# An attention and MLP layer on one core: the prologue reordered around a transposed x, and the sparse branch moved into the first head

## The chip, the cores and the metric

The program runs on one core of one Trainium2 chip. The metric is the device time of one execution in microseconds (us), as the median of several. Five engines run their own instruction streams and meet at semaphores: PE (TensorE, matmuls and transposes; PEld is its weight load), DVE (VectorE), ACT (ScalarE), POOL (GpSimd) and SP (SyncE), which here issues the DMAs. [...]

## What is computed

One transformer layer on x, 1024 tokens by 256 features, in float32:

```python
qc = layernorm(x @ W_cq, q_norm_w, q_norm_b)            # query latent, 192 wide
qp = qc @ W_q                                           # 16 heads x (128 nope + 64 rope)
kvc = x @ W_ckv                                         # 16 heads x (64 rope + 128)
kv_n = layernorm(kv_nope, kv_norm_w, kv_norm_b)
kvp = kv_n @ W_kv                                       # k_nope and v
attn = softmax(causal(q k^T * scale)) @ v               # per head, rope on q_pe and k_pe
gate = x @ W_ig;  top 8 tokens for each of 8 side heads # sparse branch
sel = rows of (x @ W_ip) at those tokens
so = softmax(sel W_sq (sel W_sk)^T / sqrt(128)) @ (sel W_sv)
attn += mean over the 8 tokens of (so @ W_io)           # one vector per side head
x = layernorm(x + attn @ W_o)
x = layernorm(x + MLP(x) with ternary weights)
```

The sparse branch gives one vector per head, the same for all tokens, so it enters the output as one row that is summed over the heads and added to all tokens.

## The kernel before

Every float32 product is made of two float32r halves, a high part (ACT or POOL rounds it, names ending in h) and a low part (DVE or POOL subtracts it, names ending in l), so a logical matmul is three matmuls (`three`, L610 to L612) and nearly every result needs an ACT copy and a DVE subtraction (the helper `lo`, L943). x is 8 tiles of 128 tokens; xTh and xTl hold its transpose in two blocks of 128 features.

Order is written by hand. One list of steps, `PROLOGUE`, then `FIRST` (heads 0 and 1), `MID` in a loop (pairs 1 to 6), `LAST` (heads 14 and 15) and `EPILOGUE` is walked by each engine, which does its own share of each step in list order and waits on semaphores for the others. A step that needs an accumulator takes one of four PSUM banks J in turn and PE waits until its last user has been read out. The scores of a head go to the two large PSUM tensors SC. Each head has 8 slots, one per query tile: `qk` (scores, L623 to L627), some filler steps, `exp`, more filler steps (transposes of the probabilities `tc`, products with v `pv`, output product `wo`, and the preparation of the next head: `kpe`, `kv`, `kvn`, `kvn2`, `kt`, `qp`, `ab`, `qn`, `ropek`, `ropeq`, `stk`, `stq`).

In the prologue the steps are: `xt` (16 PE transposes of x, L696), `qc` (the query latent and the gate for each token tile; ACT copies it out in three pieces, DVE takes statistics, L1022 and L1026), `qrs` (POOL, 1/sqrt of the variances of all 8 tiles), `kpe` and `kv` (key rope part and key/value latent of heads 0 and 1), `ropek` (POOL, L503 to L512, after a DMA swaps even and odd rows of KX), `qnorm` (DVE normalises the latent in SBUF, 16 instructions, L1033), `ab` (products of weights), `qm` (PE transposes the normalised latent; ACT scales, rounds; DVE subtracts), `side` 0 and 1 (gate transposed, top 8 by DVE), `qp`, `qn` (queries), `kvn2` and `kt` (keys of head 0), `ropeq` on DVE, and then `side` 2 to 10, the sparse branch, a chain that goes from PE to DVE and back at each of nine steps. Step 3 (L663) picks the chosen rows of x with 16 float32 matmuls of 64 columns, step 4 (L671) multiplies them by W_ip with 16 of 8 columns. At its end `rw` (the row of head 0) precedes the first `qk`. SP's DMAs `stack` copy the roped keys and queries to the doubled layouts KD, KL and QS that `qk` reads.

## Time and profile before

| | us |
|---|---|
| median of 3 executions | 739.39 (738.97 to 739.40) |
| the profiled execution | 743.51 |
| its span | 741.7 |
| first scores of head 0 (start of L623) | 84.96 |
| PE busy over the span | 670.4 (90%) |
| DVE / ACT / POOL busy | 490.9 / 397.5 / 338.9 |

The numbers of the trace are from one profiled execution, 743.51 us long, of which 741.7 us are its span; the median is 4.1 us less than that execution. Times of instructions are counted from the start of the span. In a timeline row, the first number is the start, the second the duration of the group, and what stands in brackets is the idle time before it on its engine and who ended it.

### The profile page before, as it was taken

What the parts mean: (1) busy time and instruction counts of PE and PEld (TensorE: products, weight loads), DVE (VectorE), ACT (ScalarE), POOL (GpSimd) and SP (SyncE); (2) the same over time, 40 slices, a digit from 0 to 9 for tenths busy, and PEclk for the clock granted to TensorE, in tenths of its full rate; (3) what the DMA queues carried; (4) which work ended last, traced back from release to release, by engine and by line L of the source; (5) the groups of instructions that cost most, each with busy time, mean ns of one, the idle gap of its engine ahead of it and who ended that gap; (6) DMA issues with size and microseconds to landing.
All of it is one profiled execution on the core that took longest, in us unless ns stands there. A gap on an engine that the chain in (4) does not pass through costs nothing. (4 is left out here: it accounts for less than half of the span.)

```text
span 741.7 us, 14057 instructions
## 1 busy us (share of the span) xinstructions
PE 670.4 (90%) x4416; PEld 600.9 (81%) x4416; DVE 490.9 (66%) x1401; ACT 397.5 (54%) x920; POOL 338.9 (46%) x279
## 2 busy tenths in 40 slices
PE   5667799999999999999999999999999999878994
PEld 5546699889988898899889988998899889767883
DVE  2665366666676666666766676667666668996665
ACT  3341345764576457645764476447644766644531
POOL 5622354735474547354735474547454730000443
PEclk9965599999999999999999999999999999998998
DMA  6153210551045105510541055105410545000001
GB/s 200 44 141 72 64 50 1 124 112 51 1 103 134 50 0 120 113 50 0 125 108 50 0 127 106 50 0 129 104 50 0 127 86 171 1 0 1 1 1 57
DMA packets 29486, 50.50 MB, mean 68 GB/s; under 512 B 8976, under 2 KB 20496, under 8 KB 29456
## 3 DMA queue, kind: packets, MB, share of 16 engines
q1 hardware_dynamic: 29456, 50.12, 27.0%
q8 instruction: 16, 0.26, 0.1%
q14 instruction: 14, 0.11, 0.1%
HBM read 15.50 MB, written 1.05 MB: 22 GB/s over the span
## 5 line engine op out<-in xcount | busy, mean ns | idle before, releaser
L943 DVE TENSOR_TENSOR PTl<-J,PTh 128x512 fp32r<-128x512 f32 (+1 forms) x192 | 102.2, 553 | 65.3 <-ACT PTh L832 64.7
L845 ACT ACTIVATE Pb<-SC,nm 128x128 f32<-128x128 f32 (+7 forms) x128 | 94.8, 740 | 62.9 <-DVE nm L1010 62.9
L1006 DVE CUSTOM_DVE_ANT_0 SC<-SC,mask 128x128 f32<-128x128 f32 (+7 forms) x128 | 97.3, 760 | 28.0 <-PE SC L627 25.8
L610 PE MATMUL J<-PTh,Vh 128*128 128x256 f32 x320 | 88.3, 276 | 7.0 <-DVE PTl L943 6.8
L636 PE MATMUL J<-ident,Pb 128*128 128x128 f32 x576 | 88.1, 279 | 6.0 <-ACT Pb L845 5.5
L612 PE MATMUL J<-PTh,Vl 128*128 128x256 f32 x320 | 89.3, 279 | 0.0
L611 PE MATMUL J<-PTl,Vh 128*128 128x256 f32 x320 | 89.3, 279 | 0.0
L832 ACT ACTIVATE PTh<-J 128x512 fp32r<-128x512 f32 (+1 forms) x192 | 87.5, 493 | 2.6 <-PE J L636 1.7
L636 PEld LDWEIGHTS J<-ident,Pb 128*128 128x128 f32 x576 | 63.8, 141 | 13.8 <-ACT Pb L845 5.4
L610 PEld LDWEIGHTS J<-PTh,Vh 128*128 128x128 f32 x320 | 60.7, 190 | 11.7 <-DVE PTl L943 10.4
L623 PE MATMUL SC<-KNh,QNh 128*128 128x512 f32 (+1 forms) x192 | 69.0, 360 | 0.0
L624 PE MATMUL SC<-KNl,QNh 128*128 128x512 f32 (+1 forms) x192 | 66.8, 348 | 0.0
L625 PE MATMUL SC<-KNh,QNl 128*128 128x512 f32 (+1 forms) x192 | 66.8, 348 | 0.0
L626 PE MATMUL SC<-KD,QS 128*128 128x512 f32 (+1 forms) x192 | 66.7, 347 | 0.0
L627 PE MATMUL SC<-KL,QS 128*128 128x512 f32 (+1 forms) x192 | 66.6, 347 | 0.0
L832 ACT ACTIVATE ATh<-J 128x256 fp32r<-128x256 f32 x64 | 24.5, 383 | 69.6 <-PE J L612 68.9
L611 PEld LDWEIGHTS J<-PTl,Vh 128*128 128x128 f32 x320 | 60.6, 189 | 0.7
L612 PEld LDWEIGHTS J<-PTh,Vl 128*128 128x128 f32 x320 | 60.9, 190 | 0.0
L1143 DVE SCALAR_TENSOR_TENSOR acc<-J,rs,acc 128x256 f32<-128x256 f32 x128 | 56.1, 480 | 2.6
L943 DVE TENSOR_TENSOR ATl<-J,ATh 128x256 fp32r<-128x256 f32 x64 | 27.0, 422 | 45.1 <-ACT ATh L832 45.0
L907 ACT ACTIVATE kvraw<-kvraw,nmr,rstd 128x128 f32<-128x128 f32 x128 | 52.5, 485 | 5.0 <-POOL nmr L589 5.0
L832 ACT ACTIVATE kvraw<-J 128x512 f32<-128x512 f32 x32 | 19.2, 599 | 65.8 <-PE J L612 65.8
(283 smaller groups left out, 1869.9 us busy)
## 6 DMA issues: line engine op xcount, KB each, us to landing
KD<-RKh SPq DMA_DIRECT2D x32, 256.0 KB, 4.5
KL<-RKl SPq DMA_DIRECT2D x32, 256.0 KB, 5.0
KX<-KX SPq DMA_DIRECT2D x16, 256.0 KB, 2.4
QX<-QX SPq DMA_DIRECT2D x16, 256.0 KB, 2.3
QS<-RQh SPq DMA_DIRECT2D x16, 256.0 KB, 4.0
QS<-RQl SPq DMA_DIRECT2D x16, 256.0 KB, 4.5
r_kv<-in_L_attn_W_ckv SPq DMA_DIRECT2D x8, 384.0 KB, 3.4
r_qn<-in_L_attn_W_qT SPq DMA_DIRECT2D x16, 128.0 KB, 2.8
```

The source lines that it names most:

```text
L610: mm(o, lhsT=wh, rhs=xh, start=start, stop=False)
L611: mm(o, lhsT=wh, rhs=xl, start=False, stop=False)
L612: return mm(o, lhsT=wl, rhs=xh, start=False, stop=stop)
L623: mm(o[:, k], lhsT=QNh[b][:, q], rhs=KNh[b][:, k], start=True, stop=False)
L624: mm(o[:, k], lhsT=QNh[b][:, q], rhs=KNl[b][:, k], start=False, stop=False)
L625: mm(o[:, k], lhsT=QNl[b][:, q], rhs=KNh[b][:, k], start=False, stop=False)
L626: mm(o[:, k], lhsT=QS[b][:, q], rhs=KD[b][:, k], start=False, stop=False)
L636: last = pe.transpose(o[:, tile(j - 4 * c)], Pb[i % 2][:, tile(j)], ident[:, :])
L832: return act.activation(o, i, ACT.Copy)
L845: act.activation(Pb[i % 2][:, w], SC[i % 2][:, w], ACT.Exp, bias=nm[:, i % 2:i % 2 + 1], scale=SCALE, accum_out=sm[:, b, i:i + 1]).then_in ...
L943: dve.tensor_tensor(o, i, h.bitcast(F32), ALU.subtract).then_inc(done[kind], 1)
L1006: dve.tensor_tensor_reduce(out=SC[i % 2][:, w], in0=SC[i % 2][:, w], in1=mask[:, 128 * (7 - i):S], scale=1.0, scalar=LOW, op0=ALU.add, op1 ...
```

## The change

1. The host also passes x transposed (xT), the six vectors of the two norms as one array (vec), W_cq with W_ig beside it, cos and sin as one array, and the rope columns of W_q packed for one DMA. The 16 transposes and their 4 copies disappear; xT is loaded in two halves of 512 tokens into KX, one half by SP and one by ACT's own DMA queue, which also loads cos/sin and x. Step `xs` rounds a half (ACT, 128x1024) and subtracts (DVE, 128x1024).
2. `qc` writes into SC, not into J, and is not copied out. Its statistics, `qrs` and `qnorm` are done in halves of four tiles. The first half is normalised by ACT (8 instructions out of PSUM), the second by DVE (8 instructions out of PSUM), both into QX. `qm` follows by halves.
3. The scaling of W_kvT by the norm weights and the splits of W_kvT and of the first W_q and W_o block go from POOL to a new step `w0` on ACT (copies) and DVE (one multiplication and three subtractions). It stands ahead of `kv` 0 and of the second half of `qnorm`.
4. `ropek` 0 keeps three operations on POOL; its copy and subtraction become step `rsplit` on ACT and DVE. `ropeq` 0 is done in halves on DVE with its own swap and stack DMAs.
5. Steps `side` 2 to 10 and `io` leave the prologue for the slots of head 0. The row of head 0 (`rw`) is done in the last pair, for which W_o's first block is loaded a second time.
6. Buffers of the sparse branch move from Pb to QX and Pb[1], so ACT waits for `side` 4 before it writes KX for pair 1, and for `side` 10 before it writes QX for it.

```diff
-            sp.dma_start(acc[:, :, :], x.rearrange("(t p) d -> p t d", p=128)).then_inc(ld_x, 16)
-            sp.dma_start(ident[:, :], c_ident).then_inc(ld_x, 16)
...
+            sp.dma_start(r_cq, W_cqg.rearrange("(k p) n -> p k n", p=128)).then_inc(ld_cq, 16)
+            sp.dma_start(KX[:, :, half(0)], xT.rearrange("(k p) n -> p k n", p=128)[:, :, half(0)]).then_inc(ld_xt[0], 16)
...
+            act.dma_start(KX[:, :, half(1)], xT.rearrange("(k p) n -> p k n", p=128)[:, :, half(1)]).then_inc(ld_xt[1], 16)
+            act.dma_start(CS[:, :, :], c_cs).then_inc(ld_cs, 16)
+            act.dma_start(acc[:, :, :], x.rearrange("(t p) d -> p t d", p=128)).then_inc(ld_x, 16)
...
                     if kind == "qrs":
-                        inv_std(qmv[:, :, 1], ve[:, :], rsd[:, :], qc_aggr, 1, qc_veps, qc_rstd, 1)
+                        q = slice(4 * c, 4 * c + 4)
+                        inv_std(qmv[:, q, 1], ve[:, q], rsd[:, q], qc_aggr, c + 1, qc_veps, qc_rstd, c + 1)
...
+                    if kind == "qnorm" and c == 0:
+                        act.wait_ge(qc_neg, 2)
+                        for t in range(4):
+                            v = qc_out(t)
+                            act.activation(qcm[:, t, :], v[:, 0:128], ACT.Identity, bias=nmr[:, t:t + 1], scale=rsd[:, t:t + 1])
+                            act.activation(qct[:, t, :].rearrange("p (a n) -> p a n", a=2),
...
+                    if kind == "w0":
+                        act.wait_ge(wkv_scaled, 1)
+                        copy(Wkh[:, :], r_wkv).then_inc(hi_w, 1)
+                        act.wait_ge(ld_qn, 16)
+                        copy(Wqnh[:, :, :], r_qn[:, :, :]).then_inc(wqn_hi, 1)
+                        act.wait_ge(ld_o, 16)
+                        copy(Woh[:, :], r_o[:, :]).then_inc(wo_hi, 1)
...
                     if kind == "qnorm":
-                        dve.wait_ge(qc_rstd, 1)
-                        dve.wait_ge(qc_aggr, 1)
-                        for t in range(T):
-                            for v in (qcm, qct):
-                                ins = dve.tensor_scalar(v[:, t, :], v[:, t, :], qmv[:, t, 0:1], rsd[:, t:t + 1],
...
+                    if kind == "w0":
+                        dve.wait_ge(ld_w0, LD_W0)
+                        dve.tensor_tensor(r_wkv[:, NOPE:], r_wkv[:, NOPE:], kvwr, ALU.mult).then_inc(wkv_scaled, 1)
+                        dve.wait_ge(hi_w, 1)
+                        dve.tensor_tensor(Wkl[:, :], r_wkv, Wkh[:, :].bitcast(F32), ALU.subtract).then_inc(w0_ready, 1)
...
+                add(0, first, ("side", 0, 2))
+                add(1, first, ("side", 0, 3))
+                add(2, first, ("side", 0, 4))
+                add(3, first, ("side", 0, 5), ("side", 0, 6))
+                add(4, first, ("side", 0, 7))
+                add(5, first, ("side", 0, 8))
+                add(5, last, ("wosp", 2, 0), ("io0", 0, 0))
+                add(6, first, ("side", 0, 9))
+                add(7, first, ("side", 0, 10), ("io", 0, 0))
+                add(7, last, ("rw", 2, 0))
```

The order on DVE in the prologue, before, from the statistics of the key/value latent to the low part of the first transposed query latent (Pb here holds the means, rsd the inverse deviations):

```order
L1046 BN_STATS bst<-kvraw 128x6 [waits kv_done]
L1046 BN_STATS bst<-kvraw 128x6 x3
L1033 TENSOR_SCALAR QX<-QX,Pb,rsd 128x128 [waits qc_aggr,qc_rstd]
L1033 TENSOR_SCALAR QX<-QX,Pb,rsd 128x128 x15
L1054 BN_AGGR mv<-bst 128x2 [waits bn_done]
L1054 BN_AGGR mv<-bst 128x2 x15
L943 TENSOR_TENSOR ABl<-J,ABh 128x512 [waits ab_hi]
L943 TENSOR_TENSOR qcl<-J,qch 128x512 [waits qm_hi] x2
```

And now, from the low parts of the first half to the second half of the normalisation (Pb<-Pb is the scaling of W_kvT; Wkh, Wqnh and Woh are the high parts that ACT rounds):

```order
L1012 TENSOR_TENSOR qcl<-J,qch 128x512 [waits qm_hi]
L1012 TENSOR_TENSOR qcs<-J,qcs 64x512 [waits qm_hi]
L1121 TENSOR_TENSOR Pb<-Pb 128x128 [waits ld_w0]
L1123 TENSOR_TENSOR Wkl<-Pb,Wkh 128x256 [waits hi_w]
L1125 TENSOR_TENSOR Wqnl<-r_qn,Wqnh 128x256 [waits wqn_hi]
L1127 TENSOR_TENSOR Wol<-r_o,Woh 128x256 [waits wo_hi]
L1135 BN_STATS bst<-kvraw 128x6 [waits kv_done]
L1135 BN_STATS bst<-kvraw 128x6 x3
L1106 TENSOR_SCALAR QX<-SC,Pb,rsd 128x128 [waits qc_aggr,qc_rstd]
L1108 TENSOR_SCALAR QX<-SC,Pb,rsd 128x128
```

Four operations on two SBUF inputs now stand on DVE ahead of the second half of the normalisation, which reads PSUM (SC); they were POOL's.

PE before, ahead of head 0: steps 2 to 5 of the sparse branch in one row (Pb holds the one-hot matrix and then the picked rows, KX holds W_ip):

```order
L658 MATMUL J<-i8d,onesf 128x64 [waits side_dve,qn_done]
L663 MATMUL J<-Pb,acc 128x64 [waits side_dve,qn_done]
L663 MATMUL J<-Pb,acc 128x64 x15
L671 MATMUL J<-Pb,KX 128x8 [waits ld_wip,side_done,kt_done]
L671 MATMUL J<-Pb,KX 128x8 x15
L675 MATMUL J<-Pb 128x64 [waits side_done,kt_done]
```

PE now, in the slots 0 to 2 of head 0 (SC rows are its scores, ident,Pb the transposed probabilities):

```order
L668 MATMUL SC<-KL,QS 128x128
L701 MATMUL J<-i8d,onesf 128x64 [waits side_dve,qn_done]
L664 MATMUL SC<-KNh,QNh 128x256
L665 MATMUL SC<-KNl,QNh 128x256
L666 MATMUL SC<-KNh,QNl 128x256
L667 MATMUL SC<-KD,QS 128x256
L668 MATMUL SC<-KL,QS 128x256
L677 MATMUL J<-ident,Pb 128x128 [waits exp_done,qn_done]
L707 MATMUL J<-QX,acc 128x64 [waits ld_x,side_dve,kt_done]
L707 MATMUL J<-QX,acc 128x64 x15
L664 MATMUL SC<-KNh,QNh 128x384 [waits exp_done]
```

The same matmuls of the sparse branch are issued, but after the first scores and between them, in PE's in-order queue.

## Rows read from the trace of the kernel before

**Rows 1.** Timeline of PE, 0 to 85 us: start, duration, engine, line, operation

```profile
6.70 3.67 PE L696 MATMUL J<-ident,acc 128*128 128x128 f32 x16 [6.70 <-DMA ident<-in_c_ident]
...
11.87 0.50 PE L610 MATMUL J<-KNh,xTh 128*128 128x200 f32 x1 [1.50 <-DVE xTl L943]
...
17.73 0.39 PE L610 MATMUL J<-KNh,xTh 128*128 128x200 f32 x1
...
40.87 3.65 PE L709 MATMUL J<-ident,QX 128*128 128x128 f32 x16 [10.81 <-DVE QX L1033]
...
61.41 7.06 PE L663 MATMUL J<-Pb,acc 128*128 128x64 f32 x32 [3.86 <-DVE Pb L969]
68.90 6.96 PE L671 MATMUL J<-Pb,KX 128*128 128x8 f32 x32 [0.43 <-issue]
...
81.03 0.35 PE L683 MATMUL J<-mean,Pb 64*64 64x8 f32 x2 [1.56 <-DVEq L989]
...
84.96 0.31 PE L623 MATMUL SC<-KNh,QNh 128*128 128x128 f32 x1
```

**Rows 2.** Timeline of ACT, 0 to 80 us

```profile
23.20 0.60 ACT L832 ACTIVATE KX<-J 128x512 f32<-128x512 f32 x1 [0.80 <-PE J L612]
...
52.68 3.17 ACT L907 ACTIVATE kvraw<-kvraw,nmr,rstd 128x128 f32<-128x128 f32 x8
```

**Rows 3.** Timeline of POOL, 0 to 80 us

```profile
26.98 2.40 POOL L503 TENSOR_TENSOR KX<-KX,CS 128x1024 f32<-128x1024 f32 x1 [2.90 <-issue]
...
31.77 2.34 POOL L506 TENSOR_TENSOR KX<-KX 128x1024 f32<-128x1024 f32 x1
...
42.28 2.92 POOL L554 TENSOR_TENSOR rstd<-veps,mhalf 128x16 f32<-128x16 f32 x1
...
59.99 0.72 POOL L548 TENSOR_TENSOR Wqnl<-r_qn,Wqnh 128x256 fp32r<-128x256 f32 x1
```

**Rows 4.** Groups by shape, POOL 714 to 742 us, DVE 600 to 665 us: busy, mean ns

```profile
L1226 POOL TENSOR_TENSOR rsd<-ve,mhalf 128x4 f32<-128x4 f32 x2 | 2.0, 1007 | 0.2
...
L1132 DVE TENSOR_TENSOR acc<-acc,row 128x512 f32<-128x512 f32 x4 | 2.6, 683 | 0.0
```

**Rows 5.** Timeline of DVE, 0 to 80 us

```profile
25.25 0.87 DVE L1046 BATCH_NORM_STATS2 bst<-kvraw 128x6 f32<-128x128 f32 x4 [3.27 <-ACT kvraw L832]
...
30.48 10.24 DVE L1033 TENSOR_SCALAR QX<-QX,Pb,rsd 128x128 f32<-128x128 f32 x16
40.65 1.15 DVE L1054 BATCH_NORM_AGGREGATE mv<-bst 128x2 f32<-128x6 f32 x16
...
47.95 1.28 DVE L951 COPY QX<-J 8x512 f32<-8x512 f32 x2
...
52.02 0.21 DVE L962 TENSOR_TENSOR i8d<-i8f,blk 8x64 f32<-8x64 f32 x1
56.37 1.29 DVE L943 TENSOR_TENSOR QNl<-J,QNh 128x512 fp32r<-128x512 f32 x2 [4.14 <-ACT QNh L832]
...
60.24 1.02 DVE L969 TENSOR_TENSOR Pb<-Pb,tokid 128x512 f32<-128x512 f32 x1
61.18 1.21 DVE L503 TENSOR_TENSOR QX<-QX,CS 128x1024 f32<-128x1024 f32 x1
...
65.76 1.23 DVE L512 TENSOR_TENSOR RQl<-QX,RQh 128x1024 fp32r<-128x1024 f32 x1
```

**Rows 6.** The instructions of L1033, 30 to 41 us: ns min/median/max

```profile
L1033 DVE TENSOR_SCALAR QX<-QX,Pb,rsd x16: 330/334/2501, 30.5 to 40.4; 128x128 f32<-128x128 f32 x16
```

**Rows 7.** DMA issues of the page: KB each, us from issue to landing

```profile
KL<-RKl SPq DMA_DIRECT2D x32, 256.0 KB, 5.0
```

**Rows 8.** Busy time by stretch: PE, PEld, DVE, ACT, POOL, granted clock, DMA

```profile
61.40:75.90 14.50, 14.03 (x64) 13.78 (x64) 5.57 (x7) 0.00 (x0) 0.00 (x0) 0.50 0.53 120
84.90:89.30 4.40, 4.20 (x18) 3.88 (x17) 1.87 (x8) 1.78 (x7) 3.45 (x4) 0.50 0.00 2
89.30:122.00 32.70, 32.20 (x222) 29.41 (x221) 20.35 (x57) 18.17 (x40) 17.54 (x14) 0.99 0.09 29
```

More of the change, by code:

```diff
@@ L317, in head_steps @@
             else:
+                add(0, first, ("rw", h, 0), ("wosp", n, 0))
                 add(0, more, ("qp", 1, 0), ("kvn", 1, 0))
@@ new lines, in _ @@
+            load("wkv", 0)
+            sp.dma_start(vecs[:, :], vec).then_inc(ld_vec, 16)
+            sp.dma_start(ident[:, :], c_ident).then_inc(ld_id, 16)
+            load("wqp", 0)
+            sp.dma_start(r_wkv, W_kvT).then_inc(ld_w0, 16)
+            sp.dma_start(r_wv, W_kv[:, NOPE:]).then_inc(ld_w0, 16)
+            sp.dma_start(kvwr, kv_norm_w.rearrange("(a n) -> a n", a=1).to_broadcast([128, NOPE])).then_inc(ld_w0, 16)
+            load("wqn", 0)
+            load("wosp", 0)
+            for dst, src in ((blk[:, :], c_blk), (tokid[:, :], c_tok), (off64[:, :], c_off), (mean8[:, :], c_mean)):
@@ L467, in _ @@
             sp.dma_start(wip, W_ip.rearrange("(k p) n -> p k n", p=128)).then_inc(ld_wip, 16)
-            stack("stk", 0, 0, 0)
-            sp.wait_ge(side_dve, 2)
-            swap(QX, done["qp"], 2, q_swapped)
-            stack("stq", 0, 0, 0)
+            for n, src in enumerate((W_sq, W_sk, W_sv, W_io[:, 0:128])):
+                sp.dma_start(wside[:, n, :], src).then_inc(ld_ws, 16)
             def run(steps, p):
@@ L506, in rope @@
             eng.tensor_tensor(X[:, 0, :], X[:, 0, :], X[:, 1, :], ALU.add).then_inc(mul, 1)
-            eng.wait_ge(mul, 4 * u + 3)
-            for b in range(2):
-                hold(eng, stacked[b], 96 * u)
+            eng.wait_ge(mul, 4 * n + 3)
+            if isinstance(u, int) and u == 0:
+                return
+            hold(eng, stacked[0], 96 * u - 32)
+            hold(eng, stacked[1], 96 * u)
             eng.tensor_copy(hi_[:, :], X[:, 0, :]).then_inc(mul, 1)
-            eng.wait_ge(mul, 4 * u + 4)
+            eng.wait_ge(mul, 4 * n + 4)
@@ L691, in use @@
                 b = off % 2
-                if kind == "xt":
-                    if c == 0:
-                        pe.wait_ge(ld_x, 32)
-                    for t in range(4):
-                        last = pe.transpose(o[:, tile(t)], acc[:, 4 * (c % 2) + t, tile(c // 2)], ident[:, :])
                 if kind == "qc":
                     if c == 0:
-                        pe.wait_ge(w0_ready, 1)
-                        pe.wait_ge(done["xt"], 4)
+                        pe.wait_ge(cq_ready, 1)
+                    if c % 4 == 0:
+                        pe.wait_ge(done["xs"], c // 4 + 1)
+                    o = qc_out(c)
                     for k in range(K):
-                        last = three(o[:, 0:200], xTh[:, k, tile(c)], xTl[:, k, tile(c)], Wcqh[:, k, :], Wcql[:, k, :],
+                        last = three(o[:, :], xTh[:, k, tile(c)], xTl[:, k, tile(c)], Wcqh[:, k, :], Wcql[:, k, :],
                                      k == 0, k == K - 1)
@@ L846, in run @@
                                        scale=SCALE, accum_out=sm[:, b, i:i + 1]).then_inc(exp_done, 1)
-                    if kind in ready and kind not in ("side", "wb", "wtot", "wo", "rw"):
+                    if kind in ready and kind not in ("side", "wb", "wtot", "wo", "rw", "qc"):
                         act.wait_ge(ready[kind], count(kind, u, c))
@@ L893, in run @@
+                    if kind == "rsplit":
+                        act.wait_ge(rk_mul, 3)
+                        copy(RKh[:, :], KX[:, 0, :]).then_inc(rk_mul, 1)
                     if kind == "kpe":
@@ L911, in run @@
                             wait(act, rq_ready, u)
+                        if c == 0 and isinstance(u, int) and u == 1:
+                            act.wait_ge(done["side"], 11)
                         copy(QX[:, 0, half(c)], o[:, :]).then_inc(done["qp"], 1)
@@ L1408, with attn, two @@
-    for name, a in constants().items():
-        arrays[f"in_{name}"] = np.ascontiguousarray(a)
+    args = []
+    a = {name: np.ascontiguousarray(v) for name, v in inputs.items()}
+    def attn(name):
+        return a[f"L0_attn_{name}"]
+    def two(v):
+        return np.concatenate([v, v])
+    x = attn("x").reshape(S, D)
+    qw, qb = attn("q_norm_w"), attn("q_norm_b")
+    heads = attn("W_q").reshape(QL, NP, 2, HD)
+    pe = heads[:, :, :, NOPE:].transpose(1, 0, 2, 3).reshape(NP, QL, 128)
@@ L1410 @@
+    for name in ("W_o", "W_ip", "W_sq", "W_sk", "W_sv", "W_io"):
+        arrays[f"in_{name}"] = attn(name)
+    for name in ("W_up", "W_gate", "W_down"):
+        arrays[f"in_{name}"] = a[f"L0_ffn_{name}"]
+    for name, v in constants().items():
+        arrays[f"in_{name}"] = v
+    arrays = {name: np.ascontiguousarray(v) for name, v in arrays.items()}
     for name, a in arrays.items():
```

324 lines of the change are left out of this document (184 added, 140 removed).

## The prediction

> **What bounds the kernel now.** I read the windows by stretch first, then PE's timeline, then the other engines around PE's gaps. From 89.3 us on PE is the bound: 32.20 of 32.70 us busy at a granted clock of 0.99 [rows 8], and the heads after it repeat that. So a microsecond of PE work added to a head is paid in full, and a microsecond by which head 0 begins sooner is won in full. Head 0 begins at 84.96 [rows 1]. Ahead of it PE waits in two places. First, 10.81 us for the normalised query latent: DVE takes 10.24 us for 16 small instructions [rows 5]. Second, the sparse branch, from 61.41 to 84 us. Of that, 7.06 + 6.96 us are the matmuls of steps 3 and 4, in which PE is 14.03 of 14.50 us busy, but at a granted clock of 0.50 [rows 1, 8]. The rest, about 9 us, is small steps handed to and fro.
>
> So the sum has two parts: when head 0 now begins, and by how much it gets longer.
>
> **Part 1: the begin of head 0.** *Start.* PE's 16 transposes began at 6.70 when x and ident had landed, and `qc` at 11.87 [rows 1]. xT's first half lands with 1.2 MB in flight, as x and ident did, so at 6 to 7 us; I take 7.0. ACT rounds 1024 columns (1.0 to 1.2 us, two copies of 512 at 0.60 [rows 2]), DVE subtracts 1024 (1.23 [rows 5]); `qc` begins at 9.7, some 2 us sooner.
>
> *First half of the latent.* 27 matmuls of `qc` took 5.86 us [rows 1], so 24 take 5.2: 14.9. Statistics of the last two tiles and the aggregation take 1.2 more by estimate: 16.1. POOL's power on 4 columns takes 1.0 [rows 4], with three small operations around it 1.9 by estimate: 18.0. ACT's 8 scalings cost 3.17 as those of `kvn2` [rows 2]: 21.5 with the gate copy. `kpe` is copied out behind them: 22.7 (before 23.80). The swap DMA and its wait took from 23.80 to 26.98 [rows 2, 3], so POOL's three rope operations begin at 25.9 and hold POOL until about 33.4 (three of 2.34 to 2.40 [rows 3]).
>
> *Step w0, the term that decides.* DVE finishes the low parts of `qm` 1 at 26.1 (two scalings and copies on ACT) and meets four operations with both inputs in SBUF, each 0.3 to 0.45 alone (128 and 256 columns, where 512 take 0.683 [rows 4]). The trace shows what POOL does to such work. In `qnorm` the 16 instructions have a median of 0.334 us and a longest of 2.501 [rows 6]; they took 10.24 together [rows 5] while POOL's rope ran from 26.98 on [rows 3]. L969, two SBUF inputs of 512 columns, began at 60.24, while POOL's L548 ran until 60.71; it took 1.02, where an operation of this size takes 0.683 with POOL idle [rows 3 to 5]. It ended 0.55 us after POOL's operation did, which is what its 512 elements alone need. So such an operation waits for the end of POOL's. The first of the four therefore ends at 28.4, ACT's three copies follow by 29.6, the second ends at 31.1, the third at 33.9, the fourth at 34.3. Alone the four would be through at 28.0.
>
> [...]
>
> *Second half.* Behind the four stand the statistics of `kv` 0 (0.87 [rows 5]) and `qnorm` (8 out of PSUM; from 0.33 each, as when unhindered in SBUF, overlapped to 0.3; 2.4 in all, 5 if each took twice that): 37.6. PE has been idle since about 24 and is at the lower clock. It then has 8 transposes, `kv` 1, `qp` 0, `kv` 2, `qp` 1, `kv` 3 in one row. With 0.22 a matmul at the lower clock at first (16 took 3.65 [rows 1]) and the upper clock from about 42 (as it rose at 89.3 after dense work from 84.2 on [rows 8]), that ends at 47.3.
>
> *DVE's chain.* Copy 0.6, statistics 0.9, aggregation 1.15 [rows 5]: 50.1. ABl 0.65 (half of QNl's 1.29 [rows 5]). The top 8, from 47.95 to 52.23 before [rows 5], 4.3: 55.1. Rope of the first query half, half of 61.18 to 66.99 [rows 5], 3.0: 58.1, plus 0.6 behind POOL's split of v. QNl 1.3 [rows 5]: 60.1. RKl 1.2 and about 1 behind POOL again: 62.4. The key path on POOL and ACT (power 2.92, scalings 3.17 [rows 2, 3]) ends sooner. SP then issues four stack DMAs, the last 1.9 later; it lands in 5.0 [rows 7]: **69.4**. Before, the stacks were hidden by the sparse branch; here nothing hides them. Won: 84.96 - 69.4 = **15.6 us**.
>
> **Part 2: head 0 gets longer.** *Steps 3 and 4.* PE stands idle from about 58 (the last transposes of `kt`) to 69.4, so head 0 opens at 0.50, as it did before [rows 8]. Two sets of scores (2.3 us) precede step 3. In the trace 14 us of these very matmuls left the clock at 0.50 [rows 8]. I take them at 7.06 + 6.96 = 14.0; at the upper level they would cost half. *Small steps.* Step 2 is 0.4; steps 5 to 10 are 14 matmuls of 0.11 (half of 7.06/32): 1.6. *Waits.* Step 6 waits for DVE to copy step 5, behind ABl: 1.6. Step 8 waits for the side softmax (DVE, ACT, DVE), which was 1.56 of idle PE before [rows 1] and stands ahead of `kv` and `pv` in PE's queue: 1.6. *Clock.* The scores and transposes between steps 3 and 4 now also run at the lower level, some 4 us of them: 2.0. Sum: 14.0 + 0.4 + 1.6 + 3.2 + 2.0 = **21.2 us**. The bounds are 10 (everything at the upper level, waits filled) and 25 (waits doubled).
>
> **Elsewhere.** `rw` goes from the prologue to the last pair: three matmuls and a DVE row, 0.35. POOL's W_o split now precedes `kvn` in head 1: at most 1.2, I take 0.3. The packed loads save SP issue time, which nobody waits for. The waits of ACT on step 4 and step 10 come after these in PE's order anyway. Together **+0.6**.
>
> **Sum.** -15.6 + 21.2 + 0.6 = +6.2 against the profiled 743.5, so 749.7 for such an execution. That one stood 4.1 over the median, so the median goes from 739.4 to **745.6**. Its own error, from 2 us at the start and in DVE's chain and 3 in head 0, gives 741 to 750. A difference of 0.2% (1.5 us) is about what a measurement can tell from none.
>
> **Rivals.**
> *A. The four operations of w0 aren't hindered* (they slip in ahead of POOL's rope or don't share its port). Then `qnorm` 1 ends at 31.5, RKl isn't held either: head 0 begins 7.5 sooner, +6.2 - 7.5 = -1.3, 738.1. For it: only one row of this kind of operation. Against: that row fits to 0.1 us. Chance 0.12.
> *B. Steps 3 and 4 run at the upper level.* It saves 7.0 there and about 2.5 of the scores: -3.3, 736.1. For it: in head 0 they have dense scores beside them. Against: at 61.4 to 75.9 the clock stayed at 0.50, and here it begins low. Chance 0.14.
> [...] The trace shows the clock low through 14 us of these matmuls.
> *C. Both*: +6.2 - 7.5 - 9.5 = -10.8, 728.6. Chance 0.06.
> *D. Head 0 suffers more*: the side softmax blocks DVE and with it the maxima of the scores; if each of the nine steps costs a wait like 1.56, 5 to 8 more, 752. It decides once exp of tile 5 arrives after PE has run out of `kv` work. Against: DVE is 20.35 of 32.70 us busy there [rows 8]. Chance 0.06.
> That leaves 0.62 for the forecast.
>
> **How the numbers follow.** Range 734.5 to 750.5: it leaves out C, the lower end of B and nearly all of D. The bounds of step 3 and 4 (half price) and of w0 (alone) are in it each by itself. Faster by over 0.2%: C 0.06, B 0.11, A 0.05, forecast 0.02 = 0.24. Within 0.2%: B 0.02, A 0.04, forecast 0.05 = 0.11. Slower: 0.65. The likeliest case alone: 741 to 750.
>
> **What would show it.** In the changed trace: L647 from about 9.7; POOL L522 to L525 at 26 to 33 with DVE L1123 or L1125 lasting 2 us beside them; L1106/L1108 unhindered, ending near 37.6; the first L664 at 67 to 72, released by a stack DMA; L707 and L715 of 7 us each at 0.50; PE idle before L723 and L728 of over 1 us each; head 1's first scores about 21 us further from head 0's than before. If the first L664 comes at 62, A holds; if L707 takes 3.5 us, B does. Not covered: a wait in the loop of the middle pairs, whose order is unchanged.

## The result and the profile after

| | before | after |
|---|---|---|
| median (us) | 739.39 (738.97 to 742.97, 4 executions) | 750.36 (749.26 to 750.85, 4 executions) |
| profiled execution, its span | 743.51, 741.7 | 750.04, 748.3 |
| first scores of head 0 / head 1 / head 15 | 84.96 / 120.26 / 630.07 | 72.08 / 129.27 / 637.66 |

The ratio of the times is 1.0136, 95% interval 1.0108 to 1.0163: the changed kernel is 1.4% slower. Head 0 begins 12.9 us sooner and is 57.2 us long instead of 35.3, so head 1 begins 9.0 us later. That lead shrinks to 7.6 at head 15 and to 6.6 at the end of the span.

The start of the prologue, from the timelines of ACT, DVE and PE (start, duration, engine, line, operation; in brackets the idle time before it and who ended it):

```profile
10.19 2.00 ACT L882 ACTIVATE xTh<-KX 128x1024 fp32r<-128x1024 f32 x2 [6.62 <-DMA KX<-in_xT]
...
11.28 2.99 DVE L1012 TENSOR_TENSOR xTl<-KX,xTh 128x1024 fp32r<-128x1024 f32 x2 [11.28 <-ACT xTh L882]
...
12.65 0.51 PE L647 MATMUL SC<-KNh,xTh 128*128 128x200 f32 x1 [12.65 <-DVE xTl L1012]
```

x transposed lands at 10.2, not at 7, so `qc` begins at 12.65: 0.8 us later than before (11.87 in [rows 1]), although the 16 transposes are gone.

Step w0, from the timeline of DVE, and POOL in the same stretch:

```profile
28.26 2.27 DVE L1121 TENSOR_TENSOR Pb<-Pb 128x128 f32<-128x128 f32 x1
31.02 2.01 DVE L1123 TENSOR_TENSOR Wkl<-Pb,Wkh 128x256 fp32r<-128x256 f32 x1 [0.48 <-ACT Wkh L882]
32.95 2.56 DVE L1125 TENSOR_TENSOR Wqnl<-r_qn,Wqnh 128x256 fp32r<-128x256 f32 x1
35.43 0.41 DVE L1127 TENSOR_TENSOR Wol<-r_o,Woh 128x256 fp32r<-128x256 f32 x1
35.76 0.86 DVE L1135 BATCH_NORM_STATS2 bst<-kvraw 128x6 f32<-128x128 f32 x4
36.66 0.41 DVE L1106 TENSOR_SCALAR QX<-SC,Pb,rsd 128x128 f32<-128x128 f32 x1
...
28.05 2.34 POOL L522 TENSOR_TENSOR KX<-KX,CS 128x1024 f32<-128x1024 f32 x1 [4.64 <-issue]
30.35 2.40 POOL L523 TENSOR_TENSOR KX<-KX,CS 128x1024 f32<-128x1024 f32 x1
32.82 2.40 POOL L525 TENSOR_TENSOR KX<-KX 128x1024 f32<-128x1024 f32 x1
```

Put the two engines side by side: L1121 ends at 30.53 and POOL's L522 at 30.39; L1123 at 33.03 and L523 at 32.75; L1125 at 35.51 and L525 at 35.22. Each of DVE's began while one of POOL's ran and ends 0.1 to 0.3 us behind it. L1127, of the same size as L1125, has POOL idle beside it and takes 0.41 instead of 2.56.

From there to head 0, the timelines of DVE and PE show:

```profile
39.54 1.94 PE L753 MATMUL J<-ident,QX 128*128 128x128 f32 x8 [12.91 <-DVE gts L1111]
...
51.40 1.29 DVE L1145 BATCH_NORM_AGGREGATE mv<-bst 128x2 f32<-128x6 f32 x16
...
62.73 2.17 DVE L1130 TENSOR_TENSOR RKl<-KX,RKh 128x1024 fp32r<-128x1024 f32 x1
...
72.08 0.45 PE L664 MATMUL SC<-KNh,QNh 128*128 128x128 f32 x1 [11.06 <-DMA KL<-RKl]
```

PE waits 12.91 us for the second half of the latent (before: 10.81, for the whole of it [rows 1]), and 11.06 us ahead of the first scores, for the stack DMA of RKl.

The timeline of PE in head 0:

```profile
75.36 6.93 PE L707 MATMUL J<-QX,acc 128*128 128x64 f32 x32
84.22 6.83 PE L715 MATMUL J<-QX,KX 128*128 128x8 f32 x32
...
100.79 0.41 PE L723 MATMUL J<-QX 128*64 128x128 f32 x2 [1.38 <-DVE QX L1048]
111.10 0.25 PE L728 MATMUL J<-mean,QX 64*64 64x8 f32 x2 [2.07 <-DVEq L1061]
```

And busy time by stretch (stretch, length, PE, PEld, DVE, ACT, POOL, granted clock, DMA share, GB/s):

```profile
75.30:91.00 15.70, 15.70 (x74) 15.60 (x73) 2.24 (x9) 3.43 (x10) 5.99 (x4) 0.50 0.64 152
91.00:96.00 5.00, 5.00 (x17) 4.29 (x17) 2.20 (x5) 2.58 (x4) 0.00 (x0) 0.50 0.00 0
...
98.00:125.00 27.00, 23.55 (x154) 20.61 (x153) 16.30 (x48) 10.58 (x25) 12.66 (x9) 1.00 0.11 35
```

Steps 3 and 4 (L707, L715) cost what they cost before (7.06 and 6.96, [rows 1]), at the same clock of 0.50, the lower of the two values (0.50 and 1.00) that the clock records of this case's 14 traces have. They stood ahead of head 0 and now stand in it.

### The profile page after: what moved, and what is told of

The parts are those of the page before. It is cut to its first block and busy times, and to the rows that moved or that the text cites. A ratio compares the mean times of both kernels' runs of the same rounds, so it can differ in the third digit from the quotient of the medians.

```text
span 748.3 us, 13998 instructions
## 1 busy us (share of the span) xinstructions
PE 664.8 (89%) x4400; PEld 596.8 (80%) x4400; DVE 494.8 (66%) x1403; ACT 397.5 (53%) x907; POOL 337.2 (45%) x276
## 3 DMA queue, kind: packets, MB, share of 16 engines
q1 hardware_dynamic: 24512, 48.68, 25.9%
## 5 line engine op out<-in xcount | busy, mean ns | idle before, releaser
L664 PE MATMUL SC<-KNh,QNh 128*128 128x512 f32 (+1 forms) x192 | 69.6, 363 | 11.1 <-DMA KL<-RKl 11.1
L522 POOL TENSOR_TENSOR KX<-KX,CS 128x1024 f32<-128x1024 f32 x8 | 19.1, 2386 | 77.7 <-DMA KX<-KX 73.1
```

The lines of the kernel that those rows point to most:

```text
L664: mm(o[:, k], lhsT=QNh[b][:, q], rhs=KNh[b][:, k], start=True, stop=False)
```

## The experiments

The times of the kernel before in these comparisons are from new executions on the same chip as each group. Its median was 740.2 to 741.5 there, and 739.4 beside the changed kernel. So a difference of medians between two such groups can be off by 1 to 2 us; the ratio to the kernel before doesn't have this error. The groups are: the kernel before once more, w0 earlier, loads later and the sparse branch ahead again (740.70); both edits, steps 2 to 4 ahead, the added matmuls and the 80 at the start (740.23); step 3 alone ahead and the last two rows of the table (741.51); the kernel before with PE occupied (741.05).

| kernel | median | ratio to before, 95% | head 0 begins | head 1 begins |
|---|---|---|---|---|
| before, once more | 740.42 | 1.0007 (0.9983 to 1.0031) | 82.66 | 118.36 |
| before, PE occupied from 1.4 us | 740.38 | 0.9988 (0.9971 to 1.0005) | 82.23 | 118.26 |
| after | 750.36 | 1.0136 (1.0108 to 1.0163) | 72.08 | 129.27 |
| w0 earlier | 742.75 | 1.0026 (1.0002 to 1.0049) | 63.95 | 120.78 |
| loads later | 747.19 | 1.0084 (1.0056 to 1.0111) | 68.93 | 126.08 |
| 80 matmuls added at the start | 755.73 | 1.0194 (1.0151 to 1.0237) | 78.47 | 135.03 |
| steps 3, 4 once more in head 1 | 756.18 | 1.0209 (1.0177 to 1.0240) | 70.62 | 125.47 |
| sparse branch ahead again | 750.87 | 1.0142 (1.0096 to 1.0189) | 92.23 | 127.67 |
| w0 and loads | 739.29 | 0.9979 (0.9964 to 0.9995) | 60.86 | 119.23 |
| and steps 2, 3 ahead of head 0 | 735.52 | 0.9922 (0.9906 to 0.9939) | 64.71 | 114.47 |
| and steps 2, 3, 4 ahead of head 0 | 732.44 | 0.9897 (0.9864 to 0.9930) | 68.71 | 110.41 |
| and step 3 ahead of kt | 728.48 | 0.9822 (0.9806 to 0.9839) | 65.16 | 108.74 |
| and PE occupied at the start | 726.92 | 0.9798 (0.9773 to 0.9823) | 62.86 | 106.50 |

### Step w0 moved ahead of POOL's rope

```diff
-  each("qc", 4, 5, 6, 7) + each("qrs", 1) + ... + each("qm", 0, 1) + each("w0", 0) + each("kv", 0)
+  each("w0", 0) + each("qc", 4, 5, 6, 7) + each("qrs", 1) + ... + each("qm", 0, 1) + each("kv", 0)
```

> Only the place of step w0 changes: its DVE and ACT work stands between the fourth and the fifth tile of the query latent, where POOL is idle, and no longer behind qm 1 beside POOL's rope of the shared key. Theory (DVE's instructions with two SBUF inputs wait for POOL's of 2.4 us): the four take 0.3 to 0.45 each, the second half of the latent is normalised by about 32 instead of 39.3, head 0's first scores come at 65 to 66 instead of 72.1, time 743 to 745 (-6 to -7). Rival (the cost is the handing to and fro between ACT and DVE in w0, wherever it stands): the later steps of the query latent are pushed back by as much, head 0 at 71 to 73, time 749 to 751. The second rival: head 0 comes sooner but the stacks or POOL's key path are late next: head 0 at 68 to 70, time 746 to 748.

The timelines of DVE and POOL in this kernel, then PE's first scores:

```profile
18.27 0.26 DVE L1121 TENSOR_TENSOR Pb<-Pb 128x128 f32<-128x128 f32 x1
19.01 0.43 DVE L1123 TENSOR_TENSOR Wkl<-Pb,Wkh 128x256 fp32r<-128x256 f32 x1 [0.49 <-ACT Wkh L882]
19.36 0.42 DVE L1125 TENSOR_TENSOR Wqnl<-r_qn,Wqnh 128x256 fp32r<-128x256 f32 x1
19.69 0.42 DVE L1127 TENSOR_TENSOR Wol<-r_o,Woh 128x256 fp32r<-128x256 f32 x1
...
28.66 0.41 DVE L1106 TENSOR_SCALAR QX<-SC,Pb,rsd 128x128 f32<-128x128 f32 x1
...
18.81 1.01 POOL L585 TENSOR_TENSOR rsd<-ve,mhalf 128x4 f32<-128x4 f32 x1
...
27.53 2.34 POOL L522 TENSOR_TENSOR KX<-KX,CS 128x1024 f32<-128x1024 f32 x1 [4.47 <-issue]
29.84 2.34 POOL L523 TENSOR_TENSOR KX<-KX,CS 128x1024 f32<-128x1024 f32 x1
...
63.95 0.45 PE L664 MATMUL SC<-KNh,QNh 128*128 128x128 f32 x1 [11.05 <-DMA KL<-RKl]
```

The same four instructions take 1.5 us together instead of 7.3, the normalisation ends at 31.4 instead of 39.4, and head 0 begins 8.1 us sooner. The time falls by 7.6 (by the ratios, 1.1%). All three lie a little beyond what was forecast, and both rivals fall: nothing else was late behind it. About 0.7 of the 8.1 is not w0's: the first half of the latent was through that much sooner in this trace (DVE's statistics of its last two tiles begin at 17.31, and at 18.01 in the changed kernel).

Two rows say more exactly what hinders whom. POOL wasn't idle in the new place: L1123 and L1125 ran wholly within its L585, which has 4 columns and lasts 1.01 us, and took 0.43 and 0.42. So not every POOL instruction holds DVE up until it ends; the ones that do in these traces have 256 columns or more. (The profile's spans on POOL are rough.) And the eight normalisations out of PSUM ran beside POOL's L522 and L523 here, every 0.32 us as in the changed kernel, where POOL had been idle since 35.22.

### Tables and x loaded behind the rest

```diff
-            act.dma_start(CS[:, :, :], c_cs).then_inc(ld_cs, 16)
-            act.dma_start(acc[:, :, :], x.rearrange(...)).then_inc(ld_x, 16)
...
+            sp.dma_start(CS[:, :, :], c_cs).then_inc(ld_cs, 16)
+            sp.dma_start(acc[:, :, :], x.rearrange(...)).then_inc(ld_x, 16)
             for dst, src in ((blk[:, :], c_blk), ...
```

> The rope tables and x (2.5 MB with the rest) are issued by SP behind its other loads and not on ACT's queue beside the two halves of x transposed. Theory (xT landed at 10.1 and not at 7 since it shared the DMA engines with what nobody needs yet): xT's halves land at 7 to 8, the first copy on ACT begins there, everything up to head 0 moves by 2 to 3 us, time 747.5 to 748.5. Rival (an aggregate limit or the size of xT itself sets 10 us): xT lands at 9.5 to 10.1, time 750 to 751.

Its ACT timeline:

```profile
7.36 2.00 ACT L882 ACTIVATE xTh<-KX 128x1024 fp32r<-128x1024 f32 x2 [4.79 <-DMA KX<-in_xT]
```

xT is there 2.8 us sooner, head 0 begins 3.1 us sooner, and the time falls by 3.2, 0.3 beyond the forecast. The two DMAs of 1 MB each that ACT issued at 1.3 and 1.8 us delayed the one load for which every engine waited. The two traces show it: ACT began on xT at 10.19 with the two DMAs beside it and at 7.36 without. Up to 14 us the queue of ACT's DMAs moved 2.59 MB in the changed kernel and 0.52 MB in this one; SP's half of xT landed 8.9 us after its issue there and 6.1 here.

### The sparse branch ahead of head 0 again

```diff
-                add(0, first, ("side", 0, 2))
-                add(1, first, ("side", 0, 3))
...
-                add(7, first, ("side", 0, 10), ("io", 0, 0))
...
                     each("kt", 0, 1) + each("vs", 0) +
+                    each("side", *range(2, 11)) + each("io", 0) +
```

> Sparse steps 2 to 10 and the initial output return ahead of head 0, all else as in the changed kernel. Theory (the sum of the prediction): head 0 is 35.3 long again instead of 57.2, and begins 22 to 25 us later than 72.1, at 94 to 97, since PE has nothing else beside these steps there; time 748 to 754. So placing them in head 0 gained at most 3 us. Rival 1 (the placement is what costs: waits of DVE and PE in head 0): begins at 84 to 88, time 739 to 744. Rival 2 (the placement gained much): over 756.

Head 0 is 35.4 us long again (92.23 to 127.67), and begins 20.2 us later than in the changed kernel: 750.87 against 750.36. Behind `kt` in this form, the move into head 0 neither wins nor loses. The begin at 92.23 is 1.8 us sooner than the theory had it; the time is in its range. PE stands idle for 8.66 us ahead of step 3, where it was 3.86 before [rows 1]. DVE makes the one-hot matrix only behind the rope of the queries and the low parts of the keys, from 69.82 to 70.51 in this trace:

```profile
70.61 7.06 PE L700 MATMUL J<-QX,acc 128*128 128x64 f32 x32 [8.66 <-issue]
```

### Both edits together

> Both edits together: step w0 ahead of the fifth latent tile, the rope tables and x issued by SP behind its other loads. Theory (both lie in one row ahead of head 0): the gains add, 8.2 and 3.2 us earlier in the traces so far; head 0's first scores at 60 to 61.5, time 739 to 741. Rival (the key path or the stacks take over): KNl and the stack DMAs set the begin at 62 to 63.5, time 741.5 to 743.

Head 0 begins at 60.86, so the gains add (11.2 in the trace of 8.1 + 3.1). The time is 739.29, 0.2% under the kernel before with the interval just below 1, and 11.1 under the changed kernel. With the sparse branch still in head 0, these two placements in the prologue were the whole loss.

### Steps 2, 3 and 4 in PE's idle stretch

W_ip gets 4 KB per partition of its own and the second half of KX (free once POOL has added the rotated part); the one-hot matrix, the indices and the gathered vectors stand in columns of Pb that are free then, so that the steps needn't wait for QX. The three steps leave the slots of head 0, and steps 5 to 10 stay there.

```diff
-        wip = KX[:, :, :]
+        wip0 = sb("wip0", [128, S])
+        wip = [wip0[:, :], KX[:, 1, :]]
...
-        oneh = QX[:, 0, 512:1024].rearrange("p (t n) -> p t n", t=T)
-        idxb = QX[:, 1, 0:64]
+        oneh = Pb[1][:, 512:1024].rearrange("p (t n) -> p t n", t=T)
+        idxb = Pb[0][:, 400:464]
...
-                    each("ab", 0) + each("side", 0, 1) + ...
+                    each("ab", 0) + each("side", 0, 1, 2) + ...
-                    each("kt", 0, 1) + each("vs", 0) +
+                    each("kt", 0, 1) + each("side", 3, 4) + each("vs", 0) +
```

> The two edits before, and sparse steps 2, 3 and 4 ahead of head 0: step 2 directly behind the top 8, steps 3 and 4 behind the last transposes of kt, in the stretch in which PE waits for the stack DMAs; W_ip is loaded early into space of its own and the free half of KX, one-hot, index and gathered vectors stand in free columns of Pb. Steps 5 to 10 stay in head 0. Theory (PE's idle stretch, about 11 us before the first scores, is free for 14 us of matmuls that head 0 would have to carry): head 0 is 40 to 43 long instead of 57, and begins 4 to 7 us later than without the move, at 65 to 68; time 728 to 732. Rival 1 (DVE's two operations for step 2 hold up the rope of the queries and RKl, and the clock is not up sooner): begins at 70 or later, time 733 to 737. Rival 2 (the matmuls in the gap bring the clock up early): head 0 35 to 38 long, time 724 to 727.

Head 0 is 41.7 us long (68.71 to 110.41), where 58.4 stood without the move, and begins 7.9 later (forecast 4 to 7). Together head 1 begins 8.8 sooner in the traces. The median falls by 6.9 to 732.44, 0.4 over the forecast range; the profiled executions were the slowest of the one kernel (740.37) and the fastest of the other (731.59), 8.8 apart. PE's timeline of step 3 and busy time by stretch in this kernel:

```profile
54.88 5.69 PE L710 MATMUL J<-Pb,acc 128*128 128x64 f32 x32 [1.52 <-DVE QNl L1013]
```

```profile
54.90:56.40 1.50, 1.50 (x14) 1.50 (x14) 1.50 (x2) 1.47 (x4) 0.98 (x2) 1.00 0.65 142
56.50:60.50 4.00, 4.00 (x20) 3.88 (x19) 3.75 (x7) 1.00 (x3) 0.00 (x0) 0.50 0.62 125
...
68.70:75.00 6.30, 5.96 (x28) 5.39 (x29) 2.87 (x12) 3.59 (x11) 3.19 (x3) 0.62 1.06 243
75.00:110.40 35.40, 31.43 (x211) 27.91 (x210) 21.19 (x64) 16.18 (x37) 15.54 (x11) 1.00 0.10 31
```

The clock is up within 6 us of the head's begin, where it was down for 24 us in the changed kernel. It fell in the middle of step 3, with PE busy, after a wait of 1.52 us ahead of it.

### The same with step 4 left in head 0

> As all_gap34, but step 4 (16 matmuls of 8 columns) stays in head 0, slot 2; only steps 2 and 3 stand ahead of it. The run with the same shapes in a warm head had step 3's shape at 3.7 us with the clock left at 1.00, and the clock fell to 0.50 in the middle of step 4's shape. Theory (step 4 is what keeps or takes the clock down in head 0): head 0 begins at 62 to 64 and is 48 to 52 long, its clock is not at 1.00 before step 4 has ended, time 735 to 738, 3 to 5 us over all_gap34. Rival (in head 0 step 4 costs only its own 3.5 to 4.5 us, the clock comes up without regard to it): head 0 44 to 46 long, time 730 to 732.

```profile
64.70:80.00 15.30, 15.10 (x63) 14.36 (x64) 3.57 (x13) 6.20 (x16) 5.95 (x4) 0.50 0.64 155
80.00:114.40 34.40, 31.07 (x206) 27.64 (x206) 20.53 (x63) 13.68 (x31) 12.66 (x9) 0.98 0.08 28
```

Head 0 is 49.8 us long, 8.1 more than with step 4 ahead of it, and begins 4.0 sooner. The clock is at 0.50 until step 4 has ended, with PE 15.10 of 15.30 us busy. These are the theory's numbers for the head's length and the clock; the begin at 64.71 is 0.7 later than it had it. The time is 3.1 over that of the run above, at the theory's lower end. That difference is between two groups, and by the ratios (0.9922 and 0.9897, whose intervals overlap) it is not clear of noise; the traces, with head 1 4.1 us later, carry it.

### Steps 3 and 4 in a head at the upper level

The changed kernel, with these shapes issued once more ahead of `kt` and `ab` in head 1; nothing reads them.

```diff
+                if kind in ("kt", "ab") and isinstance(u, int) and u == 2 and c == 0:
+                    pe.wait_ge(ld_cs, 16)
+                    n = 64 if kind == "kt" else 8
+                    for k in range(K):
+                        for t in range(T):
+                            mm(o[:, 64 * k:64 * k + n], lhsT=CS[:, k, tile(t)], rhs=ident[:, 0:n], start=True, stop=True)
```

> The changed kernel with the shapes of sparse steps 3 and 4 once more, in a head in which the clock is at 1.00: 16 float32 matmuls of 64 columns ahead of the kt of head 1's slots and 16 of 8 columns ahead of its ab; nothing reads their results. Theory 1 (they cost PE instructions whose length the granted clock sets, and dense neighbours keep it up): 3.5 us each at a clock of 1.00, head 1 7 us longer than 33.5, time 757 to 758. Theory 2 (such matmuls take the clock down themselves): the clock falls to 0.50 within them or behind them, 7 us each, head 1 12 to 16 us longer, time 762 to 767. Rival 3 (hidden: head 1 has spare time on PE): under 3 us.

PE's timeline, and the clock by stretch:

```profile
137.11 3.68 PE L781 MATMUL J<-ident,CS 128*128 128x64 f32 x32
...
145.34 4.53 PE L781 MATMUL J<-ident,CS 128*128 128x8 f32 x32
```

```profile
137.10:140.70 3.60, 3.60 (x34) 3.59 (x33) 2.19 (x7) 2.08 (x6) 2.68 (x2) 1.00 1.00 219
...
148.00:149.90 1.90, 1.90 (x10) 1.90 (x11) 0.54 (x2) 0.00 (x0) 1.90 (x2) 0.50 0.00 0
149.90:154.00 4.10, 4.10 (x15) 3.62 (x16) 0.69 (x1) 0.60 (x1) 2.39 (x2) 0.50 0.94 204
```

Step 3's shape goes as theory 1 has it, step 4's as theory 2. The shape of 64 columns costs half of what it costs cold (3.68 against 6.93) and leaves the clock at 1.00. In the middle of the shape of 8 columns the clock falls to 0.50 (at 147.9) and stays there through ordinary work until 154.7; PE was busy throughout. Head 1 is 42.8 us long instead of 33.5. The median is 5.8 over that of the changed kernel, less than either theory forecast: in this trace head 0 began 1.5 us sooner and was 2.3 shorter, of which more below. The clock also dipped in head 0 of the kernel with step 3 ahead of `kt` (0.92 at 85 to 90, 0.74 at 90 to 95), beside waits, so this doesn't prove that the 8-column matmuls took it down.

This same trace holds the case of rival B. Its prologue is that of the changed kernel, but the real step 4 ran from 82.76 in 3.76 us, and head 0 was 54.9 us long:

```profile
73.91 6.93 PE L707 MATMUL J<-QX,acc 128*128 128x64 f32 x32
82.76 3.76 PE L715 MATMUL J<-QX,KX 128*128 128x8 f32 x32
```

So the clock can rise there, at the same instruction stream: it did at 83.0 in this trace, and fell again at 86.4, in the last of step 4's matmuls. In five others with the branch in head 0 (after, w0 earlier, loads later, both, 80 matmuls at the start) it didn't rise, and step 4 took 6.83.

### Occupying PE at the start

```diff
+            pe.wait_ge(const_ready, 1)
+            for _ in range(80):
+                mm(J[0][:, 0:128], lhsT=onesf[:, :], rhs=onesf[:, :], start=True, stop=True)
             run(numbered(PROLOGUE), 0, [None] * NB)
```

> The changed kernel with 80 matmuls more (128 x 128, ones by ones, into a bank that is overwritten) on PE from 1.4 us, where it has nothing to do until 12.6. Theory (the changed kernel has lost the 16 transposes of x that ran from 7 to 10.5, so its first 18 latent matmuls, at 0.215 us apiece instead of 0.111, are always cold, as those of the first profile of the kernel before were and those of its second were not): the first latent matmuls come every 0.11 us, everything moves by 1.8 to 2.2 us, time 748 to 749. Rival (the clock has nothing to do with it): same cadence and the same time, 750.4 +- 0.7.

The experiment was mis-sized: each of these float32 matmuls stands in the trace as two passes (160 for the 80), they kept PE until 21.8, and `qc` began at 21.60 instead of 12.65. The time rose to 755.73. It still shows the cadence: the latent of eight tiles took 5.6 us from there, where it took 8.0 in the changed kernel.

The kernel before, with 18 of them:

> The kernel before with 18 matmuls of ones by ones on PE from 1.4 us until its transposes of x begin at about 7. So far its runs lie in two groups, about 739 and about 742 to 743.5; the first profile (743.5) had its first latent tiles 1.28 us apart, the second (739.7) 0.67 apart. Theory (which group a run falls into is set by whether the clock has risen when the latent's first matmuls run): the tiles are 0.67 apart, all runs at 738 to 740, no second group, median 0.5 to 2 us under that of the kernel before on the same chip. Rival (the spread comes from elsewhere, later in the program): two groups as before, the same median within 0.5 us.

Five of 17 executions of the kernel before beside it were over 743 us, and none of its 12 (highest 742.23), but a group at 740 to 742 remains and the medians differ by 0.7, within the interval. The first tiles are fast (a pass every 0.11 us from 12.27 on), but the matmuls also held up the transposes: DVE's first low part is at 9.64, where it was at 8.79 in the second profile of before. That the start divides the two groups of executions is not shown.

### Step 3 ahead of kt, and the same with PE occupied

```diff
-                    each("rsplit", 0) + each("ropeq", 1) + each("kt", 0, 1) + each("side", 3, 4) + ...
+                    each("rsplit", 0) + each("side", 3) + each("ropeq", 1) + each("kt", 0, 1) + each("side", 4) + ...
```

> As all_gap34, with step 3 directly behind the two matmul groups of qn, ahead of kt, and not behind kt. Theory (PE idles between these, and the low part of kt has 2 us to spare before the stacks land): step 3 from 51 to 58, step 4 from 59.5 to 66.5, first scores at 66 to 67 instead of 68.7, time 729.5 to 731. Rival (kt now comes 5 us later, KNl is late and the keys' path sets the begin): 68.5 to 70, time 732 to 733.5.

> best_order with 28 matmuls of ones by ones on PE from 1.4 us (two passes each, so 56 passes: at 0.217 and then 0.115 us they end at 9 to 9.8, where 80 of them ended at 21.8 in the run that had meant to test this and so held the latent up by 9.2 us). Theory (the first latent matmuls are cold): the 48 latent passes take 5.5 us instead of 7.3, all behind them moves by 1.5 to 2 us, time 1.5 to 2 us under best_order. Rival (the pause before xT's low part is ready, or another stretch behind, takes it back): within 0.7 us of best_order.

PE's timeline of the first of these:

```profile
52.04 3.68 PE L710 MATMUL J<-Pb,acc 128*128 128x64 f32 x32
...
65.16 0.45 PE L667 MATMUL SC<-KNh,QNh 128*128 128x128 f32 x1 [0.52 <-DMA KL<-RKl]
```

Head 0 begins 3.6 us sooner than with both steps behind `kt`, more than the 1.7 to 2.7 forecast: directly behind `qn` the clock stays at 1.00 through step 3 (52.0 to 55.7), which takes 3.68 and not 5.69. PE now waits 0.52 us for the last stack, so the two paths to head 0 are level. Head 0 itself got 1.9 us longer (43.6), with the dip of the clock in it that was told above, so head 1 begins only 1.7 us sooner, and the profiled executions are 1.8 apart (731.59 and 729.84). The medians differ by 4.0, across two groups. 728.48 is 1.8% under the kernel before.

With 28 matmuls at the start, the latent is through in 5.6 us. Busy time of its stretch in that kernel:

```profile
9.70:15.40 5.70, 5.70 (x50) 5.66 (x50) 4.47 (x14) 1.03 (x3) 4.69 (x5) 1.00 1.03 376
```

and in the changed one (what its 1.00 means is told at the end):

```profile
12.40:20.00 7.60, 7.35 (x44) 7.38 (x45) 4.13 (x12) 0.00 (x0) 4.15 (x4) 1.00 0.41 119
```

Head 0 begins 2.3 us sooner and the median is 1.6 lower, 726.92, 2.0% under the kernel before. The trace shows the theory's gain; the intervals of these two kernels overlap, so the time alone doesn't.

### The kernel before, once more

> The kernel before, unchanged, with a profile of its own: it shows where the 4.1 us lie by which the profiled execution (743.5) stood over the median (739.4). Theory 1: the first profile was slower in its start (loads, the prologue's waits); the new one has its first scores some 3 to 4 us ahead of 84.96, the heads behind it are alike, and the changed kernel's later start is then nearer to 9 us won than to 12.9. Theory 2: the difference lies in the heads (a lower granted clock for a stretch): first scores at 84.96 +- 0.5 again, and some head gaps shorter by 4 us in all. Theory 3: a profiled execution is always 4 us longer than an unprofiled one: the new profile has a span of about 741.7 again at a median of 739.4.

This profile is of an execution of 739.70 (span 737.9), 3.8 under the first. Of that, 2.3 lie ahead of head 0 (82.66 against 84.96) and 1.3 behind the begin of head 15. DVE's statistics of the latent tiles say where the first part is. The first profile, the first two and the last of eight:

```profile
14.03 0.37 DVE L1022 BATCH_NORM_STATS2 Pb<-J 128x6 f32<-128x192 f32 x1 [2.31 <-ACT Pb L832]
15.31 0.37 DVE L1022 BATCH_NORM_STATS2 Pb<-J 128x6 f32<-128x192 f32 x1 [0.91 <-ACT Pb L832]
...
20.94 0.36 DVE L1022 BATCH_NORM_STATS2 Pb<-J 128x6 f32<-128x192 f32 x1 [0.30 <-ACT Pb L832]
```

and the second:

```profile
13.45 0.37 DVE L1022 BATCH_NORM_STATS2 Pb<-J 128x6 f32<-128x192 f32 x1 [1.62 <-ACT Pb L832]
14.12 0.37 DVE L1022 BATCH_NORM_STATS2 Pb<-J 128x6 f32<-128x192 f32 x1 [0.30 <-ACT Pb L832]
...
18.14 0.37 DVE L1022 BATCH_NORM_STATS2 Pb<-J 128x6 f32<-128x192 f32 x1 [0.31 <-ACT Pb L832]
```

The first four tiles came every 1.28 us in the one and every 0.67 in the other; the last section tells why. Theory 1 holds for the larger part, with 2.3 us where it had 3 to 4: the changed kernel's later start is 10.6 us won against this profile, not 12.9.

## Why the prediction was right, and where it was off

The direction and the mechanism were right: a sooner head 0, a longer head 0, and the second larger. The median was forecast at 745.6, measured at 750.36, just inside the range (734.5 to 750.5). The forecast should have been some 4 to 5 us higher. Step by step:

| step | forecast | measured |
|---|---|---|
| x transposed landed | 7.0 | 10.2 |
| `qc` begins | 9.7 | 12.65 |
| POOL's rope | 25.9 to 33.4 | 28.1 to 35.2 |
| the four operations of w0 end | 28.4, 31.1, 33.9, 34.3 | 30.5, 33.0, 35.5, 35.8 |
| second half normalised | 37.6 | 39.4 |
| aggregation done | 50.1 | 52.7 |
| RKl done | 62.4 | 64.9 |
| head 0 begins | 69.4 | 72.1 |
| steps 3 and 4 | 14.0, clock 0.50 | 13.8, clock 0.50 |
| waits of steps 6 and 8 | 1.6 and 1.6 | 1.4 and 2.1 |
| head 0 longer by | 21.2 | 21.9 |

**What held.** *Step w0*: the row that decided, L969 in [rows 3 to 5], was the only one with two SBUF inputs, and it was enough. The 0.55 us by which it ended behind POOL's fit its 512 columns: from 512 to 1024 columns such an operation grows by 0.53 (0.683 and 1.21 [rows 4, 5]). The trace of before had more: in `qnorm` (L1033, one tensor out of SBUF) the longest instruction took 2.50 us and ended at 34.20, where POOL's L506 ended at 34.11; three more took 1.11 to 2.50 and ended within 0.1 us behind one of POOL's. So these operations with one SBUF input were held up too. In the changed kernel the four ended 2.5, 2.5 and 0.3 us apart (forecast 2.7, 2.8, 0.4), and moving them won 7.6 where rival A had been priced at 7.5. *Out of PSUM*: the eight normalisations come every 0.32 us. No row of the kernel before shows such an operation beside POOL's, so that they go unhindered (2.4 us for the eight) was the author's estimate. POOL was idle beside them in the changed kernel, so this alone doesn't test it; the run with w0 earlier does, with the same 0.32 beside POOL's rope and 2.6 us for the eight. So the prediction was right to leave them unhindered. That the two engines share a port, as rival A words it, is shown by no run; the runs show when the operations end. *Steps 3 and 4*: 7 us each at the lower clock (6.93 and 6.83 at 0.50), as [rows 8] had shown. *The waits* too.

**Term mis-sized: the start.** "xT's first half lands with 1.2 MB in flight, as x and ident did, so at 6 to 7 us." In flight were also the 2 MB that ACT's queue issued at 1.3 and 1.8 us. The measured rows run 1.5 to 3.2 us behind the forecast, and head 0 is 2.7 late. The run with the later loads had xT at 7.36 and head 0 at 68.93, against forecasts of 7.0 and 69.4, so this one term makes the 2.7. The queue on which a DMA is issued was read from the diff, but not what it adds to the bytes in flight.

**Step that failed: the base.** "That one stood 4.1 over the median, so the median goes from 739.4 to 745.6." The sum for an execution like the profiled one, 749.7, is within 0.4 of the profiled 750.04, but that is luck. Against the first profile of before, head 0 began 2.7 later than forecast and grew by 0.7 more, and what was put at +0.6 elsewhere was -2.4 (head 1 is 9.0 later, the end of the span 6.6): errors of +3.4 and -3.0. What lay in the 4.1 was slow matmuls of the first latent tiles (2.3) and something behind head 15 (1.3). The changed kernel had the first part: its PE has nothing to do until 12.65, and its first 23 latent passes came every 0.21 us and not every 0.11. In all nine traces of it and its variants in which PE has no work before the latent, 17 to 31 of the 48 passes were slow. The subtraction gave it the fast start of the other executions. Against the second profile of before the account is: head 0 10.6 sooner (82.66 to 72.08), 21.5 longer (57.2 less 35.7), -0.5 behind it (head 1 is 10.9 later, the end of the span 10.4), together +10.4; the two executions differ by 10.3.

**Elsewhere**, +0.6 was forecast, and it was -0.5 against that profile: of the +0.6 nothing is to be seen. Most of the -2.4 against the first profile thus lay in that execution of before, 1.1 of it behind head 15.

**The rivals.** A didn't happen, but the run with w0 earlier is A, and its 742.75 shows it to be worth what was said: 7.6. B happened in one trace of step 4 alone, 82.76 in 3.76 us, so a chance of 0.14 was not too high; it won 2.3 there and not 9.5, since step 3 was cold (6.93 us). C and D were not seen; the time lies 0.4 over the top of the likeliest case alone (741 to 750), and 0.1 inside the range.

**What the prediction saw and didn't follow up.** The loss was told as head 0 growing more than the prologue shrank. The runs put it otherwise: the placement in head 0 costs as much as it saves (750.87 with it undone), and the 11 us are w0 beside POOL's rope (7.6) and two loads beside the critical one (3.2). Each is the price of where one step or two loads stand.

## What to carry over

Before a step is moved to another engine or place, look at what the neighbours do in the same microseconds: DVE's operations with two SBUF inputs of 128 and 256 columns that met one of POOL's over 1024 columns ended 0.1 to 0.3 us behind it (2.0 to 2.6 us here instead of 0.3 to 0.4), while two beside POOL's 4 columns were not held up (0.43 and 0.42). Of a load that everything waits for, count all bytes that are issued before it lands, on every queue: here 2 MB on ACT's queue, issued at 1.3 and 1.8 us, put the landing of xT from 7.4 to 10.2. Where a profiled execution stands over the median, find out where the excess lies before it is taken off the forecast for the changed kernel. And a stretch in which PE waits for DMAs is the place for slow, narrow matmuls: put there they made head 0 begin 4 to 8 us later, while inside a dense head they cost 14, and the clock was at 0.50 for the first 24 us of that head.
